# A token-mixing and FFN kernel on one Trainium2 core: h moved in 32 half-size pieces from a buffer of its own, residual and bias additions later, two pieces of tile work moved

## The reference

```
attn = tanh(x @ W1 + b1)            # (16, 512, 128)
scores = attn @ v                   # (16, 512)
p = softmax(where(mask, scores, -1e30))   # 512 x 512 a sequence; mask by its type
pooled = (p @ x) / count
h = (pooled - mean) * rsqrt(var + 1e-5) * gamma + beta
w1 = (fc1_q - 128) * scales_of_128_rows   ; w2 alike
y = silu(h @ w1 + fc1_bias)
z = y @ w2 + fc2_bias
out = x + pooled + 0.5 * z
```

## Time and profile before

| | value |
|---|---|
| timed runs, median (range) | 1327.86 us (1325.63 to 1328.93) |
| profiled execution, its time | 1327.16 us |
| its span in the trace | 1325.4 us |
| TensorE busy | 1290.2 us, 97% |
| weight loads | 992.9 us, 75% |
| VectorE busy | 1069.8 us, 81% |
| ScalarE busy | 1009.2 us, 76% |
| GpSimd busy | 201.5 us, 15% |
| granted TensorE clock, whole span | 0.992 of full speed |

### The profile page before, as it was taken

The page is one execution under the profiler, slowest core; times in us unless marked ns, Lnnn a source line. Parts: engine busy times, 40 slices in busy tenths (PEclk is TensorE's granted clock), DMA queues, the critical chain, the costliest instruction groups (busy, mean ns, idle before and its releaser), DMA issues.

```text
span 1325.4 us, 20199 instructions
## 1 busy us (share of the span) xinstructions
PE 1290.2 (97%) x5851; PEld 992.9 (75%) x5851; DVE 1069.8 (81%) x2063; ACT 1009.2 (76%) x1661; POOL 201.5 (15%) x166
## 2 busy tenths in 40 slices
PE   7888999999999999999999999999999999999998
PEld 5665877777777777777777777777777777777787
DVE  6999888888788788888888788888878888888744
ACT  3676777877787887778877788877787877778775
POOL 3302111030301203011030301203021020301100
PEclk7999999999999999999999999999999999999999
DMA  7962103131140322213131230313213031230100
GB/s 226 229 217 32 65 15 66 49 64 65 29 101 1 64 65 49 81 17 66 47 64 66 35 94 1 65 66 57 72 19 80 32 64 65 38 90 1 33 32 32
DMA packets 274235, 84.54 MB, mean 64 GB/s; under 512 B 250026, under 2 KB 250692, under 8 KB 273604
## 3 DMA queue, kind: packets, MB, share of 16 engines
q1 hardware_dynamic: 272944, 82.96, 26.4%
q10 hardware_dynamic: 1172, 0.08, 0.1%
HBM read 51.47 MB, written 16.86 MB: 52 GB/s over the span
## 4 chain that ended last, share of the span: by engine, by line
PE 73%; DVE 13%; ACT 6%; issue 4%; SPq 2%; DMA 1%; ACTq 0%; DVEq 0%
PE y_ps L1182 14%; PE z_ps L1210 14%; PE y_ps L1183 13%; PE z_ps L1213 13%; PE z_ps L1212 8%; SPq L442 2%; DVE scratch L919 2%; ACT y_ps L658 2%; ACT L603 1%; DVE z_ps L972 1%; PE a_ps L1141 1%; PE a_ps L1092 1%; DVE y_lo L963 1%; PE a_ps L1093 1%; PE a_ps L1094 1%
## 5 line engine op out<-in xcount | busy, mean ns | idle before, releaser
L658 ACT ACTIVATE y_ps<-y_ps,ratio 128x512 f32<-128x512 f32 x768 | 474.1, 657 | 153.9 <-PE y_ps L1183 152.1
L1210 PE MATMUL z_ps<-w_hi,y_hi 128*128 128x512 f32 x1024 | 414.0, 404 | 11.4 <-DVE z_ps L972 7.4
L1182 PE MATMUL y_ps<-hT_hi,w 128*128 128x512 f32 x1016 | 409.2, 403 | 7.7 <-ACT y_ps L658 5.3
L1213 PE MATMUL z_ps<-w_hi,y_lo 128*128 128x512 f32 x1024 | 400.8, 391 | 0.0
L1183 PE MATMUL y_ps<-hT_lo,w 128*128 128x512 f32 x1016 | 397.5, 391 | 0.0
L963 DVE TENSOR_TENSOR y_lo<-y_f,y_hi 128x512 fp32r<-128x512 f32 x256 | 198.8, 777 | 146.1 <-ACT y_hi L571 144.9
L1210 PEld LDWEIGHTS z_ps<-w_hi,y_hi 128*128 128x128 f32 x1024 | 192.7, 188 | 84.9 <-issue 25.6
L1182 PEld LDWEIGHTS y_ps<-hT_hi,w 128*128 128x128 f32 x1016 | 191.1, 188 | 86.3 <-ACT y_ps L658 33.4
L1212 PE MATMUL z_ps<-w_lo,y_hi 128*128 128x512 f32 x640 | 249.8, 390 | 0.0
L652 ACT ACTIVATE y_f<-y_ps,vec_cols,mant 128x512 f32<-128x512 f32 x256 | 185.1, 775 | 73.8 <-PE y_ps L1183 73.4
L493 POOL TENSOR_TENSOR x<-x,scratch 128x512 f32<-128x512 f32 x64 | 91.6, 1434 | 941.6 <-ACT scratch L632 941.6
(11 more groups left out here) (207 smaller groups left out, 1166.3 us busy)
## 6 DMA issues: line engine op xcount, KB each, us to landing
x<-in_x_dram SPq DMA_DIRECT2D x64, 256.0 KB, 3.2
out_dram<-x SPq DMA_DIRECT2D x64, 256.0 KB, 2.7
x_cols<-in_x_dram SPq DMA_DIRECT2D x240, 64.0 KB, 2.2
h_cols<-scratch SPq DMA_DIRECT2D x224, 64.0 KB, 2.1
fc_codes<-in_L_ffn_fc_q_dram SPq DMA_DIRECT2D x8, 1024.0 KB, 12.5
fc_scaled<-units_dram SPq DMA_DIRECT2D x4, 1024.0 KB, 17.8
e<-powers_dram SPq DMA_DIRECT2D x3, 1024.0 KB, 15.6
h_rows<-powers_dram SPq DMA_DIRECT2D x1, 1024.0 KB, 10.8
```

The lines of the kernel that those rows point to most:

```text
L658: nc.scalar.activation(y_ps[k % 2][:], y_ps[k % 2][:], ACT.Copy, scale=ratio[:, c * NF + k:c * NF + k + 1]).then_inc(scaled, 1)
L1182: mm(o, w, hT_hi[:, c, :], start=(c == 0), stop=False, skip_group_check=True)
L1210: mm(z_ps[r][:], y_hi[k % 2][:, rows], w2_hi[:, k, :], start=(k == 0), stop=False, skip_group_check=True)
L1213: last = mm(z_ps[r][:], y_lo[k % 2][:, rows], w2_hi[:, k, :], start=False, stop=(k == NF - 1 or k in WHOLE), skip_group_check=True)
```

## The change

The change has five parts. The work of the very first sequence keeps its old form in parts 1 and 5.

1. `normalise` writes for sequences from 1 on into a view `normal` of the buffer `e1[0]`, with the features in two halves, and no longer over `pooled`. It doesn't wait for the residual additions.
2. `move_h` makes 32 copies in place of 16, 16 for features 0 to 255 and then 16 for 256 to 511, each with half the elements, on two semaphores. VectorE's transposes of chunks 2 and 3 stand in slots 25 and 26 and wait for the second.
3. GpSimd's residual additions wait for the normalised rows, its bias additions for the four splits of hT. VectorE's first transpose of x_cols, which overwrites `scratch`, waits for the residuals.
4. The high part of tile 5 is a cast on VectorE, directly ahead of its low part, and no longer one on ScalarE.
5. The low part of tile 9 stands ahead of `normalise` in slot 16; before it stood in slot 17 behind it.

```diff
-        h_moved = sem("h_moved")
+        h_moved = [sem(f"h_moved{half}") for half in range(2)]
-        DVE_MOVED = {24: [("TURNH", 0), ("TURNH", 1), ("TURNH", 2), ("TURNH", 3)], 25: [("SPLITH", 0)], 26: [("SPLITH", 1)],
+        DVE_MOVED = {24: [("TURNH", 0), ("TURNH", 1)], 25: [("SPLITH", 0), ("TURNH", 2)], 26: [("SPLITH", 1), ("TURNH", 3)],
...
+        normal = e1[0][:].rearrange("p j d -> p (j d)").rearrange("p (h j d) -> p h j d", h=2, j=NJ)
...
             def move_h(a):
-                rows = scratch[:, 0:NJ * D].rearrange("p (n d) -> p n d", d=P)
                 sp.wait_ge(h_ready, a * NJ + NJ)
-                for i in range(P // Q):
-                    for j in range(P // Q):
-                        piece = slice(j * Q, (j + 1) * Q)
-                        sp.dma_start(h_cols[piece, :, i * Q:(i + 1) * Q], rows[i * Q:(i + 1) * Q, :, piece]).then_inc(h_moved, 16)
+                for half in range(2):
+                    blocks = slice(half * 2 * NJ, (half + 1) * 2 * NJ)
+                    rows = normal[:, half, :, :].rearrange("p j (c d) -> p (j c) d", d=P)
+                    for i in range(P // Q):
+                        for j in range(P // Q):
+                            piece = slice(j * Q, (j + 1) * Q)
+                            sp.dma_start(h_cols[piece, blocks, i * Q:(i + 1) * Q],
+                                         rows[i * Q:(i + 1) * Q, :, piece]).then_inc(h_moved[half], 16)
...
             def residual(a, p, J):
-                pool.wait_ge(pooled_done, a * NJ + (J + 1))
+                if is_first(a):
+                    pool.wait_ge(pooled_done, J + 1)
+                elif J == 0:
+                    pool.wait_ge(h_ready, a * NJ + NJ)
...
             def bias(a, p, J):
                 pool.wait_ge(res_added, a * NJ + (J + 1))
-                if J == 0 and is_first(a):
-                    pool.wait_ge(hT_done, ND)
-                elif J == 0:
-                    pool.wait_ge(h_ready, a * NJ + NJ)
+                if J == 0:
+                    pool.wait_ge(hT_done, a * ND + ND)
...
-                    if i % 4 == 0:
+                    if i % 4 == 0 and i // 2 + 1 != Y_CAST:
                         y_hi_part(b, i // 2 + 1)
...
             def turn_columns(a, s, p, ch):
-                if s == 0 and by_pe(a - 1):
-                    dve.wait_ge(h_tr, a * ND)
+                if s == 0:
+                    dve.wait_ge(res_added, a * NJ)
+                    if by_pe(a - 1):
+                        dve.wait_ge(h_tr, a * ND)
...
             def normalise(a, _, p, ch):
                 for J in range(NJ):
-                    dve.wait_ge(res_added, a * NJ + (J + 1))
-                    v.tensor_scalar(pooled[J], pooled[J], mv[:, J, 0:1], rstd[1][:, J:J + 1], ALU.subtract,
+                    if is_first(a):
+                        dve.wait_ge(res_added, J + 1)
+                    o, i = (pooled[J], pooled[J]) if is_first(a) else (normal[:, :, J, :], by_halves(pooled[J]))
+                    v.tensor_scalar(o, i, mv[:, J, 0:1], rstd[1][:, J:J + 1], ALU.subtract,
                                     ALU.mult).then_inc(h_ready, 1)
...
             def turn_h(a, c, p, ch):
-                if c == 0:
-                    dve.wait_ge(h_moved, (a - 1) * 256)
+                if c % 2 == 0:
+                    dve.wait_ge(h_moved[c // 2], (a - 1) * 256)
...
+            def cast_y(b, k):
+                dve.wait_ge(silu_done, b * NF + k + 1)
+                dve.wait_ge(fc2_done, b * NF + (k - 1))
+                v.tensor_copy(y_hi[k % 2][:], y_f[k % 2][:]).then_inc(yhi_done, 1)
...
-                    if i % 4 == 1:
+                    if i % 4 == 1 and (i // 2 + 1 != Y_SOON or is_first(b)):
+                        if i // 2 + 1 == Y_CAST:
+                            cast_y(b, Y_CAST)
                         split_y(b, i // 2 + 1)
...
+                        if name == "H" and not is_first(b):
+                            split_y(b, Y_SOON)
```

More of the change, by code:

```diff
@@ L274, in build @@
         ACT_MOVED = {24: [("AFFINE", 0)], 25: [("AFFINE", 1)], 26: [("AFFINE", 2)], 27: [("AFFINE", 3)]}
-        DVE_MOVED = {24: [("TURNH", 0), ("TURNH", 1), ("TURNH", 2), ("TURNH", 3)], 25: [("SPLITH", 0)], 26: [("SPLITH", 1)],
+        DVE_MOVED = {24: [("TURNH", 0), ("TURNH", 1)], 25: [("SPLITH", 0), ("TURNH", 2)], 26: [("SPLITH", 1), ("TURNH", 3)],
                      27: [("SPLITH", 2)], 28: [("SPLITH", 3)]}
         DELAY = 4
+        Y_CAST = 5
+        Y_SOON = 9
+        Y_AT = 16
         PE_FIRST = [("USUM", 0), ("U", 0), ("DSUM", 0), ("PZ", 0), ("PZ", 1), ("PZ", 2), ("PZ", 3)]
@@ L344, in xt_buffers, with by_halves @@
             return first_xt(s) if is_first(a) else (xt_rows[s], hi[:], lo[:])
+        normal = e1[0][:].rearrange("p j d -> p (j d)").rearrange("p (h j d) -> p h j d", h=2, j=NJ)
+        def by_halves(ap):
+            return ap.rearrange("p (h d) -> p h d", h=2)
         def w1_views(k0):
@@ L917, in normalise @@
                 for J in range(NJ):
-                    dve.wait_ge(res_added, a * NJ + (J + 1))
-                    v.tensor_scalar(pooled[J], pooled[J], mv[:, J, 0:1], rstd[1][:, J:J + 1], ALU.subtract,
+                    if is_first(a):
+                        dve.wait_ge(res_added, J + 1)
+                    o, i = (pooled[J], pooled[J]) if is_first(a) else (normal[:, :, J, :], by_halves(pooled[J]))
+                    v.tensor_scalar(o, i, mv[:, J, 0:1], rstd[1][:, J:J + 1], ALU.subtract,
                                     ALU.mult).then_inc(h_ready, 1)
             def turn_h(a, c, p, ch):
-                if c == 0:
-                    dve.wait_ge(h_moved, (a - 1) * 256)
-                chunk = h_cols[:].rearrange("p (j c) n -> p j c n", j=NJ)[:, :, c, :]
+                if c % 2 == 0:
+                    dve.wait_ge(h_moved[c // 2], (a - 1) * 256)
+                chunk = h_cols[:].rearrange("p (h j c) n -> p h j c n", h=2, j=NJ)[:, c // 2, :, c % 2, :]
                 v.transpose(by_block(h_rows[:, c, :]), chunk).then_inc(h_turned, 1)
@@ L997, in ffn @@
                     for ahead, name, n in cond_steps(b, i, DVE_PLAN_FIRST if is_first(b) else DVE_PLAN, DVE_TURN, DVE_MOVED):
+                        if name == "H" and not is_first(b):
+                            split_y(b, Y_SOON)
                         steps[name](b + ahead, n, p if ahead == 2 else 1 - p, chains[ahead])
+                    if is_last(b) and i == Y_AT:
+                        split_y(b, Y_SOON)
                     if is_first(b):
@@ L1160, in transpose_h @@
                 for J in range(NJ):
-                    last = nc.tensor.transpose(a_ps[c % 2][:, J * P:(J + 1) * P], pooled[J][:, c * P:(c + 1) * P], ident[:])
+                    last = nc.tensor.transpose(a_ps[c % 2][:, J * P:(J + 1) * P], normal[:, c // 2, J, (c % 2) * P:(c % 2 + 1) * P], ident[:])
                 last.then_inc(h_tr, 1)
```

## The result

The changed kernel takes 1430.67 us (median of 4 runs, 1426.47 to 1431.36) where the kernel before takes 1328.16. The ratio is 1.077, 95% interval 1.074 to 1.079: slower by 102.5 us, 7.3 us for each of the 14 moves of h. The profiled execution took 1430.32 us, its span 1428.5 us.

The account below looks back on a forecast made before the run. TensorE, busy 97%, set the pace. 13 sequences by 7.1 + 0.7 − 0.35 = 7.45 us plus 5.7 for the last move gave 102.6, so 1327.2 + 102.6 = 1430 us; own range 1416 to 1447, 8 in 10 1395 to 1450.

Parts of the forecast that it names:

- The price of an issue: On SyncE's queue, each half-size move of h was taken at 0.70 us to issue; bounds 0.34 and 0.70.
- the equal issue times of two loads of different shape: On SyncE's queue, a load of x takes 0.347 us and one of x_cols 0.349; neither pieces nor bytes show.
- Rivals A: On SyncE's queue, a half-size issue costs half, all 32 issued in 11.2 us; 1317 to 1336 us; chance 0.13.
- B: On SyncE's queue, a half-size issue costs 0.52 us, the pace of the x_cols loads; 1353 us; chance 0.05.
- Where it lands: Second half of h lands at 621.0, so VectorE's first x_cols transpose comes 7.1 us later per sequence.
- The bias additions: GpSimd's bias adds beside VectorE's x_cols work: one meeting, 0.7 us per sequence; bounds 0 and 1.4.
- Rival C: GpSimd and VectorE meet three or more times per sequence, on top of the late moves; 1450 to 1460 us; chance 0.04.
- Tile 5: Slot 11: ScalarE's cast moved to VectorE lets the silu come earlier, gaining 0.35 us per sequence; bounds 0 and 0.36.
- Tile 9: Slot 16: low part ahead of the normalising delays the first issue of h by 0.6 us; slot 18's stall not credited.

## Why the prediction was right, step by step

The forecast was 1430 us, the measured time 1430.67. That is closer than the working deserves: the two largest terms were off, in opposite directions, and cancelled. In the traces the time from one sequence's first issue to the next one's grew by 7.48 us on average over 13 sequences (forecast 7.45), and what stands behind the last first issue by 5.6 (forecast 5.7).

**The price of an issue.** I took 0.70 us, the average spacing, for a half-size move. The changed kernel has 0.653 from start to start as a median and 0.677 on average, with one slow issue in 10 of 14 sequences (1.60 us at 724.43); the median sequence has 21.2 from first to last. The argument from the equal issue times of two loads of different shape held, and the experiments with half the pieces, half the partitions and 24 issues show it directly. Half the pieces took 18 ns off 629. Rivals A and B are refuted by the issue time alone, 0.61 to 0.65 us where they needed under 0.47 and 0.52, and the kernels with 16 and with 24 moves show that the time follows the number of issues.

**Where it lands.** I had the third transpose 23.8 us behind the first issue, 2.1 of it for landing. It came after 745.75 − 722.48 = 23.27, 1.9 for landing, and after 22.99 on average. From there to the first transpose of x_cols I had 4.98 and it took 4.99. The whole way from the first issue to that transpose is 28.26 us in this sequence, before it was 22.27: 6.0 more; on average over 13 sequences it is 27.97 for 22.38, so 5.6 more. I had 6.5 (7.1 with the 0.6 of tile 9's low part). The term was 0.9 too large.

**The bias additions.** I took one meeting, 0.7 us, and an upper bound of two, 1.4. From the first transpose of x_cols to TensorE's projection it is 755.82 − 750.74 = 5.08 us, before 3.63 (618.91 to 622.54): 1.45 more, and 1.44 on average. Both subtractions ahead of the projection met an addition, and lost 0.72 and 1.09 us; the projection had 0.4 to spare. The third, which met one too, isn't needed at slot 30. The term was 0.75 too small and lay just above its bound. Rival C had the number of meetings right, but priced the third one too. The Trainium skill ("SBUF — State Buffer", "SBUF: two separate sides") has the loser wait for the whole instruction. The trace agrees: the three subtractions end 0.54 to 0.55 us behind the addition that was running, whether that leaves 1.15 us or 1.78 for them. By that rule I should have counted every subtraction that stands beside the four additions.

**Tile 5.** I took 0.35 per sequence for the gain; slot 11's loss fell by 0.28, and alone the edit is worth 2.4 us or 0.17 per sequence.

**Tile 9.** I gave the earlier low part no credit, and charged 0.6 us for the later moves. What I didn't see is that it makes a loss also without the half moves. The normalising is also what releases the bias additions, and I moved it in the sum without asking what it then meets. In the changed kernel that loss of slot 20 is hidden, since slot 28 waits for the queue.

**The sum.** On average 5.6 for the queue and 1.44 for the bias additions; the remaining 0.45, from the projection to the next first issue, is what I had as 0.6 − 0.35 = 0.25. That makes 7.48. The clock's drop behind the wait wasn't in the sum and, as the run with the extra matmuls shows, doesn't belong there. The lower end of my own range was added up wrongly: with a spacing of 0.67 and no meeting it is 7.1 − 0.93 − 0.35 = 5.8 per sequence and about 1409 us, not 6.4 and 1416.

Of what I said would show it: 32 issues in 22 us, an idle time of 6.6 us (said: 8) before the third transpose, ScalarE and TensorE idle behind, the busy share at 92% (said: 90), slots 11 (mostly) and 18 without stalls. What I did not foresee is slot 20.

## What to carry to other kernels

Count the issues of a queue before their bytes: halving a transfer to get its first half earlier doubled the queue's time for all of it here, and can pay only while the last one still lands before its use. Ask where a full queue stops being early (here at about 23 issues per sequence, by the estimate above) and compare the change with that point. And when a step is moved that releases work on GpSimd, list every subtraction or addition of VectorE with both operands in SBUF that will stand beside that work; starting GpSimd's additions half a microsecond later cost more than the stall that the move removed.

## What the runs showed that I had not expected

- The low clock cost nothing where another engine's chain was the later one: 1432.97 us with the clock kept up, 1430.67 without. With GpSimd's work at its old times TensorE at the low clock was itself the later one at slot 30.
- SyncE's queue has one issue of 1.0 to 2.0 us in most groups of moves, of 16, 24 or 32, of unknown cause. In the changed kernel it is the third, fourth, tenth or thirteenth of its group, and four of the 14 groups have none over 1 us. How many groups have one differs between executions, and moves the time by some microseconds.
- Moving one subtraction ahead of the normalising removed a 0.41 us stall in each of 14 sequences and made the kernel 7 us slower.
